# An adapted layer and eight experts on one core: the tile load is put ahead of the store of the residual rows, and two experts' weights arrive in eighths

## The reference

```
x = x + ffn0(cond0(x))                 # first block: gathered 64x64 matrices, a spline-coded FFN 512-2048-512
h = x @ W.T + scale * (x @ A_b.T) @ B_b.T      # adapted layer, 4096 tokens x 512, adapter of rank 16 by batch row
logits = h @ gate_w.T ; take the 2 best of 8 experts, softmax of the two
y = sum over the two: share * ((silu(h @ gate_e) * (h @ up_e)) @ down_e)
out = x + y                                    # the residual of the second block is x itself
```

## Time and profile before

| what | value |
|---|---|
| median of 3 runs | 1168.5 us (1167.51 to 1172.47) |
| the profiled execution, its own time | 1163.31 us |
| its span, first to last instruction | 1161.6 us |
| mean granted TensorE clock | 0.962 of full speed |
| PE busy | 1047.1 us, 90% |
| DVE, ACT, POOL busy | 705.0, 479.6, 650.0 us |
| DMA | 188.31 MB, mean 162 GB/s |

### The profile page before, as it was taken

The page is one execution under the profiler, slowest core; times in us unless marked ns, Lnnn a source line. Parts: engine busy times, 40 slices in busy tenths (PEclk is TensorE's granted clock), DMA queues, the critical chain, the costliest instruction groups (busy, mean ns, idle before and its releaser), DMA issues. The chain is left out here.

```text
span 1161.6 us, 35512 instructions
## 1 busy us (share of the span) xinstructions
PE 1047.1 (90%) x12060; PEld 970.2 (84%) x12061; DVE 705.0 (61%) x1478; ACT 479.6 (41%) x964; POOL 650.0 (56%) x889
## 2 busy tenths in 40 slices
PE   2679999999999999869999929999999999999995
PEld 1579999989999999758889829898999999999994
DVE  8856667777766666446565724555555555555553
ACT  3246677777776676424242312222222222222221
POOL 6569889988999889503463442333333333333333
PEclk9869999999999999978999969999999999999998
DMA  6054545554554544484777467585858585844544
GB/s 257 1 162 146 179 161 185 193 190 163 184 186 167 179 161 150 157 281 126 225 235 211 154 211 218 91 217 97 229 95 230 103 223 109 209 84 79 90 79 67
DMA packets 124595, 188.31 MB, mean 162 GB/s; under 512 B 25816, under 2 KB 89432, under 8 KB 120832
## 3 DMA queue, kind: packets, MB, share of 16 engines
q1 hardware_dynamic: 55392, 130.43, 33.5%
q0 software_dynamic: 16432, 36.78, 15.7%
q10 hardware_dynamic: 52736, 20.64, 7.2%
HBM read 108.37 MB, written 81.83 MB: 164 GB/s over the span
## 5 line engine op out<-in xcount | busy, mean ns | idle before, releaser
L1723 POOL TENSOR_TENSOR idle<-small 128x1 f32<-128x1 f32 x212 | 71.6, 340 | 276.5 <-DMA out<-result,scatter_at 188.1
L1766 PE MATMUL banks<-slots,zt_hi 128*128 x568 | 189.6, 334 | 22.6 <-DVE zt_lo L1885 22.6
L962 POOL TENSOR_TENSOR in_lo<-inner,in_hi 128x512 fp32r<-128x512 f32 x128 | 175.8, 1374 | 42.5 <-ACT in_hi L1110 42.2
L1768 PE MATMUL banks<-slots,zt_lo 128*128 x568 | 184.2, 324 | 0.0
L1767 PE MATMUL banks<-slots,zt_hi 128*128 x568 | 184.2, 324 | 0.0
L1198 DVE TENSOR_TENSOR inner<-silu,banks 128x512 f32<-128x512 f32 x128 | 87.7, 685 | 125.5 <-ACT silu L1105 122.6
L1834 ACT ACTIVATE ht_hi<-banks 128x384 fp32r<-128x384 f32 x71 | 35.0, 492 | 254.5 <-PE banks L1776 246.9
L1766 PEld LDWEIGHTS banks<-slots,zt_hi 128*128 128x128 f32 x568 | 107.7, 190 | 22.8 <-issue 22.8
L1739 POOL DMA_INDIRECT out<-result,scatter_at x71 | 111.7, 1573 | 26.8 <-issue 24.4
L1767 PEld LDWEIGHTS banks<-slots,zt_hi 128*128 128x128 f32 x568 | 107.9, 190 | 0.0
L1768 PEld LDWEIGHTS banks<-slots,zt_lo 128*128 128x128 f32 x568 | 107.6, 189 | 0.0
(11 more groups left out here) (255 smaller groups left out, 3118.1 us busy)
## 6 DMA issues: line engine op xcount, KB each, us to landing
late_dram<-split_part SPq DMA_DIRECT2D x32, 816.0 KB, 4.3
slots<-late_dram SPq DMA_DIRECT2D x24, 1088.0 KB, 5.4
z_quads<-rows_dram ACTq DMA_DIRECT2D x286, 64.0 KB, 3.2
raw_part<-in_late_w SPq DMA_DIRECT2D x16, 816.0 KB, 7.3
x_t<-in_x_t SPq DMA_DIRECT2D x16, 512.0 KB, 3.3
x_both<-in_x_tok SPq DMA_DIRECT2D x16, 512.0 KB, 6.1
x_both<-in_x_res SPq DMA_DIRECT2D x16, 512.0 KB, 3.3
x1t_dram<-x_both SPq DMA_DIRECT2D x16, 512.0 KB, 6.3
```

Of the source, the lines that this page charges most:

```text
L962: nc.gpsimd.tensor_tensor(in_lo[:, cs, :], inner[u % 2][:, :, :], in_hi[:, cs, :].bitcast(F32), ALU.subtract).then_inc(in_done, 1)
L1766: nc.tensor.matmul(psum[bank][:, 0:FD], zt_hi[b][:, k, :], w_high, start=(k == 0), stop=False)
L1768: ins = nc.tensor.matmul(psum[bank][:, 0:FD], zt_lo[b][:, k, :], w_high, start=False, stop=(k == DK - 1))
```

## The change

On SP, the load of the next tile is issued ahead of the store of the residual rows. The load of the early weights, one pair of DMAs of 2176 KB before, becomes eight pairs of 272 KB: pair 0 where the whole was, pair t + 1 in SP's body(t), behind the store of tile t + 1. They go into two places in turn, so SP also waits for DVE's use of the place (`early_low`). ACT waits in body(t) for pair t instead of for the whole.

```diff
-        def load_early(sp):
+        def load_early(sp, t, b):
             for e in range(EARLY):
-                sp.dma_start(early_raw[:, e, :], io["early_w"][e]).then_inc(early_loaded, 16)
+                sp.dma_start(early_raw[:, e, PIECE * b:PIECE * (b + 1)], io["early_w"][e][:, bass.ds(PIECE * t, PIECE)]).then_inc(early_loaded, 16)
...
                 sp.wait_ge(split_stored, 32 * NT)
-                load_early(sp)
+                load_early(sp, 0, 0)
...
-            return at(0), at(1), early_raw[:, e, bass.ds(PIECE * t, PIECE)]
+            return at(0), at(1), early_raw[:, e, PIECE * b:PIECE * (b + 1)]
...
                 def body(t, n, b, has_next, first):
                     if has_next:
-                        store_out(t + 1)
                         if not (isinstance(t, int) and t == LNT - 2):
                             next_x1(t + 2)
+                        store_out(t + 1)
+                        if not (first and b == 0):
+                            sp.wait_ge(early_low, EARLY * t)
+                        load_early(sp, t + 1, 1 - b)
+                next_x1(1)
                 store_out(0)
-                next_x1(1)
...
-                    act.wait_ge(early_loaded, 16 * EARLY)
+                    act.wait_ge(early_loaded, 16 * EARLY * (t + 1))
...
-                                if not has_next:
-                                    ins.then_inc(weights_loaded, LOADS)
+                                ins.then_inc(*((early_low, 1) if has_next else (weights_loaded, LOADS)))
```

More of the change, by code:

```diff
@@ L384, in build @@
         adapted_layer(nc, alloc, sem, psum, ident, small, idle, lower, ones, tok_ids, out_tiles, x1, x1_loaded, load_x1,
-                      w_hi, w_lo, a_hi, a_lo, adapter_scale, chosen, rows_dram, kc["c_blank"], weights_loaded, slots, early_raw, early_loaded, staging, x_both, ctl, expert_f, ctl_ready, lent_xa_hi, lent_xa_lo)
+                      w_hi, w_lo, a_hi, a_lo, adapter_scale, chosen, rows_dram, kc["c_blank"], weights_loaded, slots, early_raw, early_loaded, load_early, staging, x_both, ctl, expert_f, ctl_ready, lent_xa_hi, lent_xa_lo)
         layer.close()
@@ L1249, in adapted_layer @@
 def adapted_layer(nc, alloc, sem, psum, ident, small, idle, lower, ones, tok_ids, out_tiles, x1, x1_loaded, load_x1,
-                  w_hi, w_lo, a_hi, a_lo, adapter_scale, chosen, rows_dram, blank_rows, weights_loaded, slots, early_raw, early_loaded, staging, x_both, ctl, expert_f, ctl_ready, lent_xa_hi, lent_xa_lo):
+                  w_hi, w_lo, a_hi, a_lo, adapter_scale, chosen, rows_dram, blank_rows, weights_loaded, slots, early_raw, early_loaded, load_early, staging, x_both, ctl, expert_f, ctl_ready, lent_xa_hi, lent_xa_lo):
     with ExitStack() as scope:
@@ L1288, in adapted_layer, with early_piece @@
         x1t_high, x1t_low, xa_split, xa_done, idle_done = (sem(n) for n in ("x1t_high", "x1t_low", "xa_split", "xa_done", "idle_done"))
-        tok_turned, out_stored, early_high = sem("tok_turned"), sem("out_stored"), sem("early_high")
-        def early_piece(t, e):
+        tok_turned, out_stored, early_high, early_low = sem("tok_turned"), sem("out_stored"), sem("early_high"), sem("early_low")
+        def early_piece(t, b, e):
             at = lambda l: slots[:, e, bass.ds(l * HALF_W + PIECE * t, PIECE)]
-            return at(0), at(1), early_raw[:, e, bass.ds(PIECE * t, PIECE)]
+            return at(0), at(1), early_raw[:, e, PIECE * b:PIECE * (b + 1)]
         chosen_set, step, both_ready = sem("chosen_set"), sem("route_step"), sem("both_ready")
@@ L1466, in body @@
                     copy(t, b, 1, 1)
-                    act.wait_ge(early_loaded, 16 * EARLY)
+                    act.wait_ge(early_loaded, 16 * EARLY * (t + 1))
                     for e in range(EARLY):
-                        to, _, raw = early_piece(t, e)
+                        to, _, raw = early_piece(t, b, e)
                         nc.scalar.activation(to, raw, ACT.Copy).then_inc(early_high, 1)
@@ L1586, in body @@
                             for e in range(EARLY):
[L1587 removed]
+                                hi, lo, raw = early_piece(t, b, e)
                                 dve.wait_ge(early_high, EARLY * t + e + 1)
                                 ins = nc.vector.tensor_tensor(lo, raw, hi.bitcast(F32), ALU.subtract)
[L1590 to L1591 removed]
+                                ins.then_inc(*((early_low, 1) if has_next else (weights_loaded, LOADS)))
                     if is_last(t):
```

## The result

| | before | changed |
|---|---|---|
| median of 5 runs each, same chip | 1170.41 us (1167.51 to 1172.47) | 1157.7 us (1156.32 to 1162.6) |
| ratio of the times | | 0.9913, interval 0.989 to 0.9937 |
| profiled execution, its span | 1163.31, 1161.6 | 1156.32, 1154.6 |
| mean granted clock of TensorE | 0.962 | 0.964 |

The change makes the kernel 0.9% faster by the ratio of all runs; the medians lie 12.7 us apart.

A forecast was written before the change was run, and what follows sets the result against it. Bound: a loop through SP's one queue (store, x1 load), then ACT and DVE. T(7) = 528.5 + 6 x 20.1 = 649.1 against 647.7, 1.4 us later; median 1168.5 + 1.4 = 1169.9 us, range 1159 to 1179.

The forecast's parts named there:

- Together 8.6: DMA engines, tile 1: residual store 5.5 us plus x1's 1 MB load 3.1 us, times simply adding up.
- the prediction's own equation: Early pair's landing E behind T, when DVE has turned a tile: 15.7 us, taken as 15.6; loop 20.1 us.
- the store's own loop: DVE's next turn waits for the residual store, landing 12.8 us behind T; 5.75 more make 18.6 us a tile.
- The check on two tiles: Adding up engine times for x1's landing in the kernel before closed within 0.4 us on two tiles.
- T(1) 15.75 us behind T(0): Tile 0: DVE has turned tile 1 at 528.5 us, after the store's landing at 522.75; 2.6 us earlier than before.
- about half of the engines for the row stores: POOL's row stores each use 0.68 us of DMA engines every 1.35 us, so take 0.50 while they last.
- PE's 18.3 us a tile: What PE itself needs per tile, read from a tile of the kernel before in which it hardly idled.
- The last tile's late pair: Tile 7: the last early pair lands about T + 8.4, perhaps late for ACT; cost 0 to 0.5 us, taken as 0.
- The 8.6 us by which PE should have come ahead: Tile 0: earlier x1 saves PE 5.6 us of stall and 3.0 us of lowered clock.
- (a): Rival: early pair isn't the last link; store's loop or PE gives 18.3 to 18.6 us tiles, -7.9 us, 1160.6; chance 0.20.
- (c): Rival: store behind the load takes only 2.8 us, PE alone holds 18.3 us tiles, -9.4 us, 1159.1; chance 0.06.
- (b): Rival: residual store loses out to POOL's row stores; tiles of 21.7 us, +11 us, 1179.5; chance 0.24.

The follow-up runs named there:

- swap_only: Kernel before with only SP's order changed: x1's load ahead of the residual store, early weights loaded whole; 1155.42 us against 1168.82, ratio 0.9881.
- pair_twice: Changed kernel with every early pair loaded twice, the first copy to columns that nobody reads; 1178.77 us, ratio 1.0092.
- pair_ahead: Changed kernel with each early pair issued one tile sooner, ahead of x1 and the store; 1156.89 us, ratio 0.9897.
- ahead_halves: `pair_ahead` with the first x1 loaded in halves, the first once DVE has turned two parts of tile 0; 1156.6 us, ratio 0.9899.
- after_again: The changed kernel itself, measured once more beside the swap alone; 1161.33 us, ratio 0.9923.
- wide_512: Kernel before with the residual store written to a scratch tensor by four DMAs of 128 partitions in 512-byte runs; 1161.76 us in one run.

## Why the prediction was wrong

**The step that failed** is the price of store and load together, "Together 8.6", carried from the old order to the new one. In the new order they take 7.35 us (`swap_only`, tile 1). Put into the prediction's own equation, E - 1.4 = 7.4 + 1.45 + 0.5 (E - 7.15) gives E = 13.3 instead of 15.7 and a loop of 13.3 + 4.5 = 17.8 us instead of 20.1. PE needs about 18, so the loop drops under it and the tile is PE's. Measured were 12.95 to 13.4 in tiles 3 to 5 and 18.08 us as the mean tile. A microsecond in the price becomes two in the tile, since the row stores take half of the engines for as long as it lasts. That the corrected sum meets the measured landing is no proof that each of its terms is right: SP's issues, the last at T + 7.2 to 7.7 in these tiles, and the 5.4 to 5.8 us from there to the landing give the same moment. That a 0.56 MB pair more costs both issue and landing time says that the engines' time is part of it.

I had taken the rate of 188 GB/s as a property of the store wherever it stands in the queue. With the same price too high, the store's own loop (12.8 + 5.75 = 18.6 us) was wrong as well: in the changed kernel and in `swap_only` DVE waited for the store in tile 0 alone. The check on two tiles could not catch it: both had the old order too. Such a check tells that the sum closes, not that its terms survive the move. (One reading of it was a little off: the store's first bytes moved at T + 1.0, not T + 1.4. The end at T + 10.0, on which the sum rests, stands.)

**What was right.** T(1) 15.75 us behind T(0): measured 15.72, with DVE waiting for the store until T + 10.1 as forecast (10.0). Part of that is luck: the last store was issued only at T + 4.0 and landed 6.1 us later, so there the issue sets the landing as much as the bytes do. The waits for x1 are gone but for tile 0, as forecast. The pair as the last thing in the queue, with a loop of landing + 4.5 us (4.8 in `pair_twice`), and about half of the engines for the row stores (2.4 to 3.6 us for a second pair, 2.9 by the sum). PE's 18.3 us a tile (17.8 in `pair_ahead`, where nothing else waits). The last tile's late pair was foreseen and too small: 0 to 0.5 us forecast, 1.35 measured. It landed at T + 10.2 and not 8.4, with two row stores of tile 6 (1.6 us of the engines) left out of the sum, and SP's issues.

**Tile 0.** I had PE's stall under 1 us and the clock at 1.00. It was 1.85, with the clock down for 4 us. x1 landed at T + 7.1 (522.64 - 515.54) and not 5.3: its second half was issued at T + 1.1 and took 6.0 us, where I had put the shortest landing of the trace before, 4.1. The 4352 KB taken from in front of it gave nothing (`swap_only`). The 8.6 us by which PE should have come ahead were 5.2: the product behind the stall began at T(0) + 8.6 (524.12 - 515.54) instead of + 12.5 (525.19 - 512.71), and the clock gave back 3.0 - 1.7. The time does not hang on it, since the store's loop sets T(1) (`ahead_halves`: no wait for x1, T(1) 1.3 us nearer by the sooner store, and no gain in the whole that the runs can tell).

**The rivals.** (a) is what happened: the pair is not the last link because load and store overlap better than I added them, tiles of 18.08, a little under its 18.3, and -10.8 us in the layer where it gave -7.9. Of (c), the tile time is right and the reason is not: behind the load the store is not 2.8 us, the two together fell by 1.25. (b) is refuted as the rule, but the profiled execution of `after_again` comes within its reach in one tile (21.75 against its 21.7).

**The rule on 512 bytes.** `wide_512` moves 279 GB/s in the store's part, with the runs that moved 188 over 32 partitions. "DMA: Bandwidth & Descriptors" (Specifications) of the Trainium skill has 512 bytes as enough for line rate. The trace of before seemed to speak against that; the experiment says that the runs were not the main fault, which is nearer to the page than the prediction was. But 2 KB runs over 128 partitions went at 362, so 512 bytes were not enough for the full rate here, and no run reached the page's ceiling.

**Open.** Why 1 MB of load directly ahead lets the 32-partition store share the engines, while a store ahead (224 GB/s) or a 0.56 MB pair ahead (252) does much less: the landings show the overlap, no row shows the resource. How much of the three scratch stores' speed is their shape and how much their addresses: a store of the real residual over 128 partitions was not tried. And whether a late pair is made by the row stores behind T or by SP's issues.

## What to carry to other kernels

When a queue holds a load that the next step needs and a store that nobody needs soon, issue the load first: here two swapped lines gave the whole gain, and the finer loads around them gave nothing. A transfer's price holds for its place in the queue; before carrying it through a reordering, treat the sum of the two as unknown by at least the part in which the engines were not full. Where a loop's length and the busiest engine's lie within 10% of each other, a microsecond in one term decides which of them the time follows, so give the two cases near equal chances.

## What the runs showed of the hardware

- The same 2.1 MB, a load of 1 MB and a store of 1 MB in one queue: 8.6 us store first, 7.35 load first (tile 1, `before` and `swap_only`).
- 1 MB stored by four DMAs at the head of the queue: 188 GB/s with 32 partitions and 512-byte runs, 236 with 32 partitions and 8 KB runs, 279 with 128 partitions and 512 bytes, 362 with 128 partitions and 2 KB (191, 219, 273 and 336 from the first bytes). The last three wrote to a scratch tensor.
- SP's issue of four stores took 3.4 to 4.0 us in the kernel before and 4.0 to 5.1 in the changed one, that of two x1 loads 2.3 to 4.1 and then 1.2 to 1.6: what stands behind in the queue is issued more slowly, not what it is.
- The granted clock fell to 0.62 and 0.53 behind a PE stall of 1.85 us in tile 0, to 0.73 and 0.70 behind one of 2.69 in `ahead_halves` (tile 1), to 0.50 behind one of 3.00 in tile 0 of `swap_only`, and to 0.50 behind one of 2.65 in tile 2 of `after_again`. It stayed at 1.00 behind one of 2.86 in tile 2 of the kernel before, and behind one of 3.01 in tile 0 of `pair_twice` (1.00 from 518 to 531). So the length of a stall alone does not tell whether the clock falls. Nor does its place: PE had idled 4.26 us at the layer's start in each of these kernels, and that ended 8 us before the stall both in `swap_only`, where the clock fell, and in `pair_twice`, where it did not. What tells the cases apart is open.
